# Rows of scores and their biases half a tile later in two engines' lists of a two-layer cross-attention kernel

## What is computed

```
q, k, v = h1 @ wq, h1 @ wk, h1 @ wv             # all rounded to 8 bits
sim  = fq(q) . fq(k) * SCALE                    # 16 heads x 1024 x 1024 for each of 4 batches
attn = softmax(sim)                             # then rounded to 8 bits, step 1/255
out  = fq(attn) . fq(v);  x = out @ wo + bo + x
x = cross_attention(ln(x), context) + x         # 77 keys, 8-bit rounding
x = (a * gelu(g)) @ ff_w2 + ff_b2 + x           # first layer ends
hidden = x + rope_attention(rms(x), rms(context)) @ Wo
y = hidden + (silu(n @ Wgate) * (n @ Wup)) @ Wdown
```

## Time and profile before

| | |
|---|---|
| median of three runs | 2611.18 us (2611.0 to 2615.15) |
| profiled execution, whole time | 2606.43 us |
| its span, first to last instruction | 2604.6 us |
| PE busy | 2006.9 us (77%) |
| DVE busy | 1807.6 us (69%) |
| ACT, POOL busy | 1137.0 us, 944.2 us |
| mean granted clock of TensorE | 0.872 of full speed |

### The profile page before, as it was taken

How to read it: one execution, slowest core, us unless ns; L and a number is a source line. 1 busy time by engine, 2 the same in 40 slices (tenths; PEclk the granted TensorE clock), 3 DMA queues, 4 the chain that set the end, 5 groups by cost and what they waited for, 6 DMA issues and landing times.

```text
span 2604.6 us, 41636 instructions
## 1 busy us (share of the span) xinstructions
PE 2006.9 (77%) x10552; PEld 1439.3 (55%) x10552; DVE 1807.6 (69%) x3327; ACT 1137.0 (44%) x1906; POOL 944.2 (36%) x1628
## 2 busy tenths in 40 slices
PE   3556477978788787888788787878787787878786
PEld 2323255655556565656556565656555565656665
DVE  1456768677777868677877868677777868685532
ACT  1234453545344553545454554545353545444211
POOL 1213334344443434343443434343433424343212
PEclk8666688999989898998989898998889898989888
DMA  7577453453636353443536363543545353634010
GB/s 234 114 133 145 90 120 73 82 123 75 129 73 133 63 123 74 97 106 74 130 73 132 65 135 61 104 99 74 121 73 124 66 130 60 129 60 105 9 40 4
DMA packets 749785, 251.18 MB, mean 96 GB/s; under 512 B 661244, under 2 KB 742896, under 8 KB 749360
## 3 DMA queue, kind: packets, MB, share of 16 engines
q1 hardware_dynamic: 746287, 249.54, 45.6%
q10 hardware_dynamic: 3328, 0.01, 0.1%
HBM read 88.62 MB, written 22.40 MB: 43 GB/s over the span
## 4 chain that ended last, share of the span: by engine, by line
PE 39%; DVE 18%; issue 16%; SPq 12%; ACT 6%; DMA 5%; POOL 3%; DVEq 1%; ACTq 0%; POOLq 0%
PE work L1389 17%; PE work L1399 14%; SPq L541 4%; DMA PT<-Pn 3%; ACT E L894 3%; DVE scaled_row L1050 3%; PE rowps L1460 3%; DVE Pn L1057 2%; PE outps L1445 2%; DVE hids L1197 1%; POOL scs L794 1%; SPq L532 1%; DVE st L1073 1%; DMA xa<-in_x 1%; DVE xs L1187 1%
## 5 line engine op out<-in xcount | busy, mean ns | idle before, releaser
L1050 DVE TENSOR_SCALAR_CACHE_REDUCE scaled_row<-rowps,der 128x1024 uint8<-128x1024 f32 x512 | 654.6, 1279 | 322.8 <-PE rowps L1460 322.6
L894 ACT ACTIVATE E<-rowps,ebias,der 128x1024 f32<-128x1024 f32 x512 | 615.2, 1203 | 405.0 <-DVE scaled_row L1050 311.4
L1057 DVE TENSOR_SCALAR Pn<-E,rowinv 128x1024 int16<-128x1024 f32 x512 | 390.9, 764 | 164.1 <-DMA PT<-Pn 140.1
L728 POOL TENSOR_TENSOR rowden<-rowsum,raw 128x1 f32<-128x1 f32 x512 | 118.7, 232 | 957.5 <-ACT E L894 956.2
L1460 PE MATMUL rowps<-KC,QP 16*128 16x512 bf16 x1024 | 219.7, 426 | 242.1 <-ACT E L894 232.1
L731 POOL TENSOR_TENSOR rowinv<-rowden,minus 128x1 f32<-128x1 f32 x512 | 332.0, 648 | 91.6 <-POOL rowden L728 91.6
L1460 PEld LDWEIGHTS rowps<-KC,QP 16*128 16x128 bf16 x1024 | 49.0, 92 | 410.6 <-ACT E L894 281.6
L1389 PE MATMUL work<-hTs,ff_w_sb 128*128 128x256 f32 x1024 | 263.8, 413 | 13.0 <-ACT hTs L870 13.0
L1389 PEld LDWEIGHTS work<-hTs,ff_w_sb 128*128 128x128 f32 x1024 | 204.6, 206 | 60.4 <-issue 16.0
L1554 PE MATMUL work<-K,hids 128*128 128x154 f32 x1024 | 156.3, 305 | 28.8 <-DVE scs L1211 18.8
L1554 PEld LDWEIGHTS work<-K,hids 128*128 128x128 f32 x1024 | 141.4, 194 | 46.2 <-DVE scs L1211 25.1
(11 more groups left out here) (142 smaller groups left out, 3281.2 us busy)
## 6 DMA issues: line engine op xcount, KB each, us to landing
VW<-vw_dram SPq DMA_DIRECT2D x32, 640.0 KB, 4.8
K<-k_dram SPq DMA_DIRECT2D x16, 616.0 KB, 4.2
KC<-k_dram SPq DMA_DIRECT2D x128, 64.0 KB, 2.4
VB<-v_dram SPq DMA_DIRECT2D x64, 128.0 KB, 3.2
PT<-Pn SPq DMA_TRANSPOSE x512, 3.1
V<-v_dram SPq DMA_DIRECT2D x16, 320.0 KB, 3.9
vw_dram<-scs SPq DMA_DIRECT2D x32, 154.0 KB
K<-k_dram SPq DMA_DIRECT2D x16, 308.0 KB, 3.1
```

What stands on the lines that cost most here:

```text
L728: nc.gpsimd.tensor_tensor(rowden[:, n:n + 1], rowsum[:, n:n + 1], raw[:, DW1:DW1 + 1], ALU.mult).then_inc(row_den.sem, 1)
L894: nc.scalar.activation(E[:, slot, :], rowps[n % 2][:], ACT.Exp, bias=ebias[:, n:n + 1], scale=der[:, AL1:AL1 + 1], accum_out=rowsum[:, n:n ...
L1050: nc.vector.tensor_scalar(scaled_row[:, n % 2, :], rowps[n % 2][:], der[:, NAL1:NAL1 + 1], 3.0e38, ALU.mult, ALU.min, accum_out=ebias[:, n ...
L1057: nc.vector.tensor_scalar(Pn[:, n % 2, :], E[:, ring(n)[0], :], rowinv[:, n:n + 1], 255.0, ALU.mult, ALU.min).then_inc(row_round.sem, 1)
```

## The change

In PE's list, `row(n + 2)` moves from the top of tile n to behind the chain work of half 2n. In DVE's list, B and R change places around `until(2 * n)`: before, tile n is R(n-1), half 2n, B(n+2), half 2n+1; now it is B(n+1), half 2n, R(n-1), half 2n+1. The order of the B's and R's among themselves stays (R(n-1) still stands before B(n+2)), and so does the order of the rows; both streams slide by half a tile against the chain work of their engine. The lists of ACT, POOL and SP are the same instruction for instruction.

```
             if not parts["old"]:
-                for n in range(AHEAD):
-                    biggest(n)
+                biggest(0)
             for n in range(ROWT):
+                if tiles(parts, n + 1):
+                    biggest(n + 1)
+                beside.until(2 * n)
                 if tiles(parts, n - 1):
                     rounded_probs(n - 1)
-                beside.until(2 * n)
-                if tiles(parts, n + AHEAD):
-                    biggest(n + AHEAD)
                 beside.until(2 * n + 1)
...
             for n in range(ROWT):
+                beside.until(2 * n)
                 if tiles(parts, n + AHEAD):
                     row(n + AHEAD)
-                beside.until(2 * n)
                 if (n - LAG) % 4 == 3 and tiles(parts, n - LAG):
                     values((n - LAG) // 2 - 1)
                 beside.until(2 * n + 1)
```

## The result

| | before | after |
|---|---|---|
| median | 2611.09 us (2607.67 to 2615.15) | 2683.9 us (2676.95 to 2690.27) |
| ratio, 95% interval | | 1.0278 [1.0248, 1.0307] |
| profiled span | 2604.6 us | 2688.5 us |
| mean granted clock | 0.872 | 0.841 |

A forecast was written before the change was run, and what follows sets the result against it. No single engine bounds throughout: SP's queue from `down` to `wo`, then a DVE chain, then mostly PE. (a), (b), (d) +41, (f), (g) −16, (h) +4: +29 on 2606.4, in run medians 2640 us; range 2590 to 2670.

The forecast's parts named there:

- the steps for SP: From `down` to `wo`, SP's queue without a wait sets `wo`, so a later xns makes `wo` 1.3 us later.
- the sum per full step: Delays added over a full step: (a) 1.3, (b) 1.0, (c) 0, (d) 0.7 and (h) 0.3 us.
- (d): Second layer norm: xs starts 0.7 us later, pieces from xs to xns the same in sum; bounds 0 and +1.4.
- (c): From the projection after `wo` to row 20: gains and delays sum to 0; bounds −1.2 and +0.5 us.
- (h): Clock: more matmul time at 1.2 GHz after waits, +0.3 us a step, +4 in all; bounds −20 and +20.
- (a): `down` to `wo`: one more B ahead of xns makes `wo` 1.3 us later, 17 over 13 steps; bounds 0 and 2.0.
- (b): `wo` to the next projection: xs 1.4 us later, the projection 1.0 later, 14 over 14 steps; bounds +0.5 and +1.4.
- PE catches up inside the stretch: Between `down` and `wo`, PE makes up its delay, then stands some 3.6 us at `wo`.
- (e): R moves away from its transposes: its DMA waits, 140 us in all, mostly go, but the time gains nothing.
- (f): Step 0: set-up matmuls run beside E, tiles take 3.6 us for 4.43, −11 over 13 tiles; bounds 0 and −24.
- (g): Step 1: the same pattern as step 0 in places, −5 us; bounds 0 and −15.
- Rival 4: The clock: all steps take the long form, +20 us, and (a) reaches 2.0, giving 2670 us; chance 0.08.

The follow-up runs named there:

- new_6_9_fill: before_fill with the new order in tiles 6 to 9 alone, around `wo`; 2559.4 us.
- before_fill: The kernel before the change with short unneeded bf16 matmuls in PE's waits; 2549.1 us.
- after_fill: The changed kernel with short unneeded bf16 matmuls ahead of seven waits of PE; 2616.7 us.
- fill_tr1: The changed kernel with 18 short matmuls in PE's wait ahead of tr1 and none elsewhere; 2651.0 us.
- old_22_25: The changed kernel with the old order of rows, B's and R's in tiles 22 to 25, around the second layer norm; 2625.6 us.
- dve_only: The kernel before with only DVE's half of the change, PE's rows left as before; 2664.4 us.
- old_26_28: The changed kernel with the old order in tiles 26 to 28, around `down`; 2691.9 us.
- b25_behind_xns: The changed kernel with one pair swapped per step, B(25) behind xns of the second layer norm instead of ahead; 2683.6 us.

## Why the prediction was right or wrong

The sign was right and the steps for SP held; the size was off by 44 us. The step that failed is the sum per full step, +3.3 where 7.2 came, and in it three terms: (d), 0.7 where 1.8 came, because it let `xns` keep its length; (c), 0 where 2.1 came (2.5 up to `wo2`); and (h), the clock, 0.3 where 1.6 stand behind tr1 alone. (a) had the right size, 1.2 for 1.3, and (b) was too large, 0.1 for 1.0. Of the signs named beforehand, PE's waits for exponentials fell to 197 us and not below half of 232, its wait at `wo` is some 2.5 us in most full steps and not over 3, and the full steps take 150.5 to 154.5 us, not 145.5 to 151. Term by term:

**(a) `down` to `wo`: right in full steps, wrong in the others.** B(29) and the sum, and then SP's store and last `oT<-OS`, and `wo`:

```profile
1268.07 1.28 DVE L1050 TENSOR_SCALAR_CACHE_REDUCE scaled_row<-rowps,der 128x1024 uint8<-128x1024 f32 x1
...
1269.27 0.69 DVE L1186 TENSOR_TENSOR xns<-work,xs 128x512 f32<-128x512 f32 x1
```

```profile
1310.01 1.84 DMA oT<-OS
1311.85 0.14 issue
1311.98 3.35 PE work L1398 x8
```

xns starts 3.4 us after `down` (2.2 before, forecast 3.6), `wo` 0.1 after its landing and 46.2 after `down` (forecast 45.5). But in the last four with "low" but no "pre", where SP has less to issue, the distance went from 39.4 to 40.2 up to 43.4 to 44.1, and PE does not wait at `wo`. I had carried 1.3 there too; the 4 us are PE's, its waits ahead of rows 2 and 6 (3.96 and 4.05, where 1.93 and 0.48 stood). "PE catches up inside the stretch" was the wrong cover for these steps, since waits don't only vanish when rows stand later: rows pair up, and PE has nothing left to do until the exponential of the first of the pair frees a buffer.

**(b) `wo` to q2: the delay of xs is there, its price is not.** In full steps xs starts 1.4 us later after `wo`, as worked out, but the projection only 0.1 for 1.0; in the steps without "pre" xs is 0.3 earlier (3.8 for 4.1). With filled waits, new_6_9_fill has it 2.2 later, of which 0.3 is left at `wo2`.

**(c) q2 to row 20: put at 0 with +0.5 as its upper bound, measured 2.1,** and 1.6 between the filled kernels. I had counted places in DVE's list and nothing else. Part of it is the clock's. In the steps whose stretch from 19 to 50 us behind `wo` has at most 1.3 us at 1.2 GHz, tr3 starts at 48.3 in before_fill (steps 5, 6, 9 and 11) and at 49.2 in after_fill (7 and 10): 1.0 us is the order's. In the steps of after_fill where tr3 starts at 52.1, the matmuls `VW,pTs` on the way there are at 1.2 GHz for a part; here they are in step 5 and then in step 6:

```profile
857.48 4.58 PE L1398 MATMUL work<-VW,pTs 128*128 128x256 f32 x20
```

```profile
1005.10 6.37 PE L1398 MATMUL work<-VW,pTs 128*128 128x256 f32 x20
```

The delay is there early. By 39 us behind `wo`, ahead of the second block of these matmuls, all of the 2.1 us are lost. On the way PE waits 1.8 us for POOL's `pps` of L803 where it waited 0.2, and 0.9 for DVE's `pTs` where it waited 0.4 (means of steps 4 to 10). What in DVE's list holds these two up was not run.

DVE's order also changes how long operations take, which I did not look for. POOL's cast `pps<-p` of L779 takes 0.70 us in all 64 instances before; after, it takes 1.05 in 60, and in each of these R runs beside it, where before B did or nothing. Before, POOL, and after, POOL and DVE:

```profile
1326.62 0.70 POOL L779 CAST pps<-p 128x616 bf16<-128x616 uint8 x1 [3.89 <-DVE p L1119]
```

```profile
1367.62 1.05 POOL L779 CAST pps<-p 128x616 bf16<-128x616 uint8 x1 [4.62 <-DVE p L1118]
...
1367.37 0.75 DVE L1057 TENSOR_SCALAR Pn<-E,rowinv 128x1024 int16<-128x1024 f32 x1
```

R ends 0.49 us into the cast. The Trainium skill, "SBUF — State Buffer", section "Who interferes with whom", calls the ports that DVE and GpSimd share "an exclusive lock": a tensor_scalar that writes out its accumulator, as B does, doesn't take them, and one without, as R, can. This trace agrees. The casts are not the cause of (c), though: the first of a step starts some 49 us behind `wo`, when the 2.1 us have been lost. What they cost further on was not run by itself.

**(d) Second layer norm: +0.7 with a bound of +1.4, measured 1.8.** xs starts 0.9 us later after `wo2` (3.5 for 2.6), nearly as worked out, and "the pieces from xs to xns are the same in sum" held: xns starts 4.92 us behind xs, 4.96 before. B(25) stands ahead of it in both, before with R(23) between them, now right in front. What I had not counted is that xns itself grew by 1.0 us, in each of steps 2 to 14. DVE before:

```profile
1206.68 1.28 DVE L1050 TENSOR_SCALAR_CACHE_REDUCE scaled_row<-rowps,der 128x1024 uint8<-128x1024 f32 x1
...
1208.49 0.77 DVE L1057 TENSOR_SCALAR Pn<-E,rowinv 128x1024 int16<-128x1024 f32 x1
1209.18 0.72 DVE L1087 TENSOR_SCALAR xns<-xs,mv,rs 128x256 f32<-128x256 f32 x2
```

After, DVE and then POOL:

```profile
1243.33 1.28 DVE L1050 TENSOR_SCALAR_CACHE_REDUCE scaled_row<-rowps,der 128x1024 uint8<-128x1024 f32 x1
...
1244.54 1.71 DVE L1086 TENSOR_SCALAR xns<-xs,mv,rs 128x256 f32<-128x256 f32 x2
```

```profile
1244.83 1.27 POOL L826 TENSOR_TENSOR hids<-hids 128x512 f32<-128x512 f32 x1
```

The first of the two tensor_scalar takes 0.4 us in both kernels, the second 0.4 before and 1.4 after: it ends 0.15 us behind POOL's product `hids`, which before started only at 1210.00, when xns was over. So the sum of the pieces was right and the length of one of them was not.

**(e)** held: R's waits went and nothing came of it.

**(f), (g) The first steps.** Step 0 gave 9.0 us, predicted 11; its tiles 16 to 25 take 3.7 us for 4.0 by the starts of their exponentials (forecast 3.6), as the 4.43 of the earlier trace rows was one tile taken for all. Step 1 lost 1.2, where a gain of 5 had been expected.

**(h) The clock: +0.3 a step, measured several times that.** Behind tr1, PE lost another 1.6 us on the way to `down` (6.1 against 4.5 in the table), the 3.78 us above. With filled waits this loss is gone: 9.8 us from tr1 to `down` in after_fill, 9.7 in before_fill. The part that fill_tr1 gives back is 33 us. Rival 4 put the clock at 20 us in all, with steps going over to the long form of 147.2; it did not think of a still longer form, and 153.6 is one. The Trainium skill, "TensorE: Matmul & The Clock Gate", Part 1, says that activity releases the throttle; the filled kernels, 61 to 67 us faster for more work, agree. But the reading drawn from it in the prediction, that collected waits would be what speaks against the change, does not carry the 73 us: 68 are there with the waits filled, and at least 45 of them can't be the clock's.

What stays open: 12 of the 68 us, which no place alone shows (3 of the 56 in full steps); what in DVE's list makes the 1.0 us of (c) that is the order's; and why tiles 22 to 25 are worth 58 us without the matmuls and only 4 to 20 with them.

## What to carry to other kernels

When a stream is slid against other work, list the pairs that come together as well as the waits that go: where two items of a double-buffered stream stand back to back, the third waits for the whole loop, with no work between them to hide it. Don't take the length of an operation as fixed either: here a new neighbour on POOL made two short DVE operations 1.0 us longer. Follow it through the lists that the change doesn't touch, too, since a copy behind an exponential on ACT inherits every delay of the stream. And price an order of instructions twice, once as it is and once with short matmuls in TensorE's waits; here this told most of an order's cost (68 us) from the clock's (61 to 67), and the second could be had for a few unneeded matmuls.

## What the hardware showed that was not expected

- A few unneeded bf16 matmuls in seven or eight waits per step made either order 61 to 67 us faster (2610 to 2549, 2684 to 2617, 2598 to 2535; by the ratios 59 to 63).
- Step lengths are not spread evenly. In after, old_22_25, fill_tr1 and dve_only 40 of the 52 steps from 2 to 14 are within 0.5 us of one of 143.3, 146.8, 150.2 and 153.6 us, and many repeat to 0.1. dve_only has steps of 146.9 and of 153.6 with one and the same list. A microsecond gained in a step may thus show as nothing (old_26_28, b25_behind_xns) or as 3.4 (fill_tr1). Why they settle there is not shown here.
- xns (two tensor_scalar of 128x256, float32) took 0.72 us before the change and 1.71 with POOL's `hids` product beside it, all of it in the second of the two; POOL's cast 0.70 beside B and 1.05 beside R.
- A float32 matmul of 256 columns is recorded as two, 0.216 us apart at the full clock.
